# Counting graph edges on VectorE: window staging moved off GpSimd, digit sums moved three groups later

## What is computed

```python
deg = maximum(segment_sum(ones, dst), 1); d = deg ** -0.5
h = relu(layernorm(x))
feat = h
for i in range(10):
    agg = segment_sum(feat[src] * (d[dst] * d[src])[:, None], dst)
    feat = (agg * 0.9 + 0.1 * h) * r[i] + (1 - r[i]) * feat
x = x + feat
emb = relu(layernorm(x))
for _ in range(4):
    m = (emb @ W_msg.T + b_msg).reshape(n, 4, 128)
    emb = gru(segment_sum(m[src, edge_type], dst), emb, ...)
return x + emb
```

## Time and profile before

| | us |
|---|---|
| median of three runs | 2482.77 (2481.85 to 2486.41) |
| the profiled execution's own time | 2481.51 |
| its span in the trace | 2480.0 |
| PE busy | 2164.4 (87%) |
| VectorE (DVE) busy | 1392.8 (56%) |
| ScalarE (ACT) busy | 502.2 (20%) |
| GpSimd (POOL) busy | 236.5 (10%) |

### The profile page before, as it was taken

The page is one execution under the profiler, slowest core; times in us unless marked ns, Lnnn a source line. Parts: engine busy times, 40 slices in busy tenths (PEclk is TensorE's granted clock), DMA queues, the critical chain, the costliest instruction groups (busy, mean ns, idle before and its releaser), DMA issues.

```text
span 2480.0 us, 40786 instructions
## 1 busy us (share of the span) xinstructions
PE 2164.4 (87%) x14375; PEld 1409.1 (57%) x14886; DVE 1392.8 (56%) x2707; ACT 502.2 (20%) x1119; POOL 236.5 (10%) x517
## 2 busy tenths in 40 slices
PE   1645555499999999999799999999999999999997
PEld 1323222388998989888544465444654446544464
DVE  6878788677777777777732246322464224642243
ACT  0868778510000000000310012100121000210000
POOL 1756556100000000000000000000000000000000
PEclk9656556599999999999899999999999999999998
DMA  2000000000000000003200000000000000000001
GB/s 75 12 32 22 32 21 29 30 24 2 2 2 2 2 2 2 2 2 109 85 1 1 1 1 1 1 1 1 1 1 1 1 1 1 1 1 1 1 1 52
DMA packets 22185, 34.31 MB, mean 14 GB/s; under 512 B 2450, under 2 KB 18442, under 8 KB 21469
## 3 DMA queue, kind: packets, MB, share of 16 engines
q1 hardware_dynamic: 19025, 30.56, 3.6%
q10 hardware_dynamic: 2944, 0.93, 0.2%
HBM read 18.04 MB, written 13.45 MB: 13 GB/s over the span
## 4 chain that ended last, share of the span: by engine, by line
PE 77%; DVE 8%; ACT 6%; issue 4%; DMA 2%; ACTq 1%; DVEq 1%; POOL 1%; POOLq 0%
PE ps L852 42%; PE ps L771 26%; PE ps L804 3%; ACT weighed L516 3%; PE ps L792 2%; ACT packed L509 2%; ACT words L498 1%; ACTq L489 1%; DVE marks L1038 1%; DVE dig L1066 1%; DVE big L1068 1%; DMA big<-in_L_gnn_w_hh 1%; DMA x_after_hops<-x 1%; PE ps L712 1%; PE ps L668 1%
## 5 line engine op out<-in xcount | busy, mean ns | idle before, releaser
L852 PE MATMUL ps<-slots,m_parts 125*128 125x500 fp8e4 (+1 forms) x5600 | 1083.8, 353 | 1.4 <-DVE slots L1338 1.0
L852 PEld LDWEIGHTS ps<-slots,m_parts 125*128 125x128 f16 x5600 | 546.5, 98 | 488.2 <-issue 0.8
L771 PE MATMUL ps<-parts,big 125*128 125x256 f16 x6125 | 669.6, 273 | 6.2 <-DVEq L1385 4.0
L771 PEld LDWEIGHTS ps<-parts,big 125*128 125x128 fp8e4 x6125 | 591.2, 98 | 63.5
L1338 DVE TENSOR_SCALAR slots<-big 128x3200 int32<-128x3200 int32 (+1 forms) x112 | 244.1, 2183 | 280.4 <-PE ps L852 280.4
L668 PE MATMUL ps<-hot_pair,weighed 125*128 125x228 f16 x1000 | 209.9, 358 | 207.6 <-ACT weighed L516 121.7
L668 PEld LDWEIGHTS ps<-hot_pair,weighed 125*128 125x128 f16 x1000 | 113.4, 120 | 303.9 <-ACT weighed L516 266.3
L516 ACT ACTIVATE weighed<-marks,win_w 125x128 f16<-125x128 f16 x625 | 195.5, 389 | 121.0 <-DVE marks L1038 119.9
L1440 DVE SCALAR_TENSOR_TENSOR r_parts<-ps,over,r_parts 128x500 f16<-128x500 f32 (+1 forms) x28 | 19.1, 683 | 230.1 <-ACT r_parts L586 230.1
L1447 DVE SCALAR_TENSOR_TENSOR gate_r<-ps,over,gate_r 128x500 f32<-128x500 f32 (+1 forms) x28 | 19.1, 682 | 228.6 <-PE ps L804 228.6
L462 ACT ACTIVATE rs<-rs 125x25 f32<-125x25 f32 x3 | 0.7, 224 | 716.1 <-DVE rs L917 716.1
(11 more groups left out here) (203 smaller groups left out, 1329.8 us busy)
## 6 DMA issues: line engine op xcount, KB each, us to landing
packed_counts<-packed SPq DMA_DIRECT2D x16, 625.0 KB, 2.9
big<-packed_counts SPq DMA_DIRECT2D x4, 1600.0 KB, 7.3
big<-packed_counts SPq DMA_DIRECT2D x3, 1200.0 KB, 6.5
hd<-in_x SPq DMA_DIRECT2D x1, 1562.5 KB
x_again<-in_x SPq DMA_DIRECT2D x1, 1562.5 KB
x_after_hops<-x SPq DMA_DIRECT2D x1, 1562.5 KB
big<-x_after_hops SPq DMA_DIRECT2D x1, 1562.5 KB
out<-big SPq DMA_DIRECT2D x4, 250.0 KB
```

What stands on the lines that cost most here:

```text
L771: last = pe.matmul(ps[:, n % RING, 0:2 * F], tot_f8[0:Q, c, a, :], both((parts0, parts1)[par], a), start=a == 0, stop=a == TILES - 1)
L852: last = pe.matmul(ps[:, k % 2, 0:SIZES[k] * Q], m_parts[0:Q, a, h, t * F:(t + 1) * F], slots_f8[0:Q, t % 2, 0:SIZES[k], a, 0:Q], start=a ...
```

## The change

GpSimd's `stage_window` and its loop are gone. Two tables are made once by ScalarE, before the counting: `tab_two` (both tables of `tab`, each element twice) and `tab_w` (the weights in f32). VectorE loads `lo` itself, forms `win_key`, and reads places and weights in `tab_two` by the register's address; ScalarE loads `lo` too, and reads its weight per partition in `tab_w` by the register's address. VectorE's wait for `s_wst` is now one for its own key operation, behind `marks`. The digit sums move: `sum_digits(blk - 2)` stands behind the second group of block `blk`, ten groups behind the last one-hots that it sums; blocks 0 and 1 of one-hots stand ahead of the loop, blocks 2 to 13 in three turns of it, and 14 and 15 behind it. `sum_digits(14)` now comes behind the statistics, right ahead of `sum_digits(15)`. ScalarE parts its lanes one group earlier (j = 2, 3, 4).

```diff
@@ buffers
-            win_place = sb("win_place", [128, DEPTH, W, 2], F16, b)
-            win_f = sb("win_f", [128, DEPTH, W, 2], F16, b)
-            win_w = sb("win_w", [128, DEPTH, W], F32, b)
+            tab_two = sb("tab_two", [128, 2, PAD, 2], F16, b)
+            tab_w = sb("tab_w", [128, PAD], F32, b)
@@ gpsimd
-            def stage_window(q, b):
...
-            with pool.Fori(0, Q // DEPTH) as i:
-                for j in range(DEPTH):
-                    stage_window(DEPTH * i + j, j)
-            for q in range(Q // DEPTH * DEPTH, Q):
-                stage_window(q, q % DEPTH)
@@ scalar
             act.wait_ge(s_prep, 1)
             act.wait_ge(s_wout, 1)
 
+            act.wait_ge(s_trc, 3)
+            for j in range(2):
+                ins = act.activation(tab_two[0:CH, j, :, :], tab[0:CH, j, :].rearrange("p (k o) -> p k o", o=1)
+                                     .broadcast_to([CH, PAD, 2]), ACT.Copy)
+            ins.then_inc(s_two, 1)
+            act.activation(tab_w[0:CH, :], tab[0:CH, 1, :], ACT.Copy).then_inc(s_two, 1)
...
+            act.wait_ge(s_two, 2)
+
             def weigh(q, b):
+                lo = act.value_load(windows[0:1, ds(q, 1)], min_val=0, max_val=NCH)
                 act.wait_ge(s_marks, q + 1)
                 for w in range(WA):
                     act.activation(weighed[0:CH, b, w, :], marks[0:CH, b, w, :], ACT.Copy,
-                                   scale=win_w[0:CH, b, w:w + 1]).then_inc(s_weighed, 1)
+                                   scale=tab_w[0:CH, ds(lo + w, 1)]).then_inc(s_weighed, 1)
...
-                    if 3 <= j < 3 + LANES and turn_before is not None:
-                        part_lane(turn_before, 1 - b, j - 3, 16 * turn_before + BQ * (1 - b) + BQ - 1)
+                    if 2 <= j < 2 + LANES and turn_before is not None:
+                        part_lane(turn_before, 1 - b, j - 2, 16 * turn_before + BQ * (1 - b) + BQ - 1)
...
-            part_lane(NB // 2 - 1, 0, 2, BQ * (NB - 1) - 1)
@@ vector, onehots
                 many = dve.value_load(windows[0:1, ds(q + MANY, 1)], min_val=0, max_val=NCH)
-                dve.wait_ge(s_wst, q + 1)
+                lo = dve.value_load(windows[0:1, ds(q, 1)], min_val=0, max_val=NCH)
+                weights_from = nc.s_assert_within(lo + WA, 0, PAD - WD)
+                TT(win_key[0:CH, b, :, :], keys[0:CH, ds(lo, W)].rearrange("p (w o) -> p w o", o=1).broadcast_to([CH, W, 2]),
+                   q_off[0:CH, ds(q, 1)].rearrange("p (w o) -> p w o", o=1).broadcast_to([CH, W, 2]),
+                   ALU.subtract).then_inc(s_wst, 1)
                 dve.wait_ge(s_hot_used, q + 1)
...
                 TT(by_two(marks[0:CH, b, :, :], 128), row(iota_row[0:CH, :], W, 128),
-                   each(win_place[0:CH, b, :, :], W, 128), ALU.is_equal).then_inc(s_marks, 1)
+                   each(tab_two[0:CH, 0, ds(lo, W), :], W, 128), ALU.is_equal).then_inc(s_marks, 1)
+                dve.wait_ge(s_wst, q + 1)
                 TT(by_two(hot_pair[0:CH, b, :, :], KP), row(iota_pair[0:CH, :], W, KP),
                    each(win_key[0:CH, b, :, :], W, KP), ALU.is_equal).then_inc(s_pairs, 1)
                 dve.wait_ge(s_marks, q + 1)
                 TT(by_two(weighed[0:CH, b, WA:W, :], 128), by_two(marks[0:CH, b, WA:W, :], 128),
-                   each(win_f[0:CH, b, WA:W, :], WD, 128), ALU.mult).then_inc(s_weighed_d, 1)
+                   each(tab_two[0:CH, 1, ds(weights_from, WD), :], WD, 128), ALU.mult).then_inc(s_weighed_d, 1)
@@ vector, order
-            for j in range(BQ):
-                onehots(j, j % DEPTH)
-            def block_of(blk, b):
-
-                for j in range(BQ):
-                    onehots(BQ * (blk + 1) + j, j % DEPTH)
-                    if j == BQ - 2:
-                        sum_digits(blk, b)
+            dve.wait_ge(s_two, 2)
+
+            def block_of(blk, b, n=BQ):
+
+                for j in range(n):
+                    onehots(BQ * blk + j, j % DEPTH)
+                    if j == 1:
+                        sum_digits(blk - 2, b)
+
+            for j in range(2 * BQ):
+                onehots(j, j % DEPTH)
...
-            sum_digits(NB - 2, 0)
             dve.wait_ge(s_wout, 1)
...
             root_of(stats[0:Q, :, 1], EPS)
+            sum_digits(NB - 2, 0)
             sum_digits(NB - 1, 1)
             one_over_root(rstd[0:Q, :], 1)
```

More of the change, by code:

```diff
@@ L269, in build @@
         s_wst, s_pairs, s_hot_used = sem("window_staged"), sem("pair_onehots_made"), sem("onehots_used")
+        s_two = sem("tables_doubled")
         s_marks, s_weighed = sem("place_onehots_made"), sem("place_onehots_weighed")
@@ L1043, in onehots @@
                 TT(by_two(weighed[0:CH, b, WA:W, :], 128), by_two(marks[0:CH, b, WA:W, :], 128),
-                   each(win_f[0:CH, b, WA:W, :], WD, 128), ALU.mult).then_inc(s_weighed_d, 1)
+                   each(tab_two[0:CH, 1, ds(weights_from, WD), :], WD, 128), ALU.mult).then_inc(s_weighed_d, 1)
                 with dve.If(many > 0):
-                    lo = dve.value_load(windows[0:1, ds(q, 1)], min_val=0, max_val=NCH - 1)
+                    first = dve.value_load(windows[0:1, ds(q, 1)], min_val=0, max_val=NCH - 1)
                     with dve.Fori(0, many) as j:
@@ L1049, in onehots @@
                         dve.wait_ge(s_more_used, dve.snap(made))
-                        col = nc.s_assert_within(lo + j + W, 0, PAD - 1)
+                        col = nc.s_assert_within(first + j + W, 0, PAD - 1)
                         TS(win_x[0:CH, 0:1], keys[0:CH, ds(col, 1)], q_off[0:CH, ds(q, 1)], None, ALU.subtract)
@@ L1100, in onehots_general @@
                            ALU.is_equal, ALU.mult).then_inc(s_more_g, 1)
-            for j in range(BQ):
-                onehots(j, j % DEPTH)
-            def block_of(blk, b):
-                for j in range(BQ):
-                    onehots(BQ * (blk + 1) + j, j % DEPTH)
-                    if j == BQ - 2:
-                        sum_digits(blk, b)
-            with dve.Fori(0, (NB - 2) // ROUND) as i:
+            dve.wait_ge(s_two, 2)
[5 more added lines that the diff above has]
+            for j in range(2 * BQ):
+                onehots(j, j % DEPTH)
+            TURNS = (NB - 3) // ROUND
+            with dve.Fori(0, TURNS) as i:
                 steps.loop(i, 4 * ROUND)
                 for k in range(ROUND):
-                    block_of(ROUND * i + k, k % 2)
-            steps.done((NB - 2) // ROUND)
-            for blk in range((NB - 2) // ROUND * ROUND, NB - 2):
+                    block_of(ROUND * i + k + 2, k % 2)
+            steps.done(TURNS)
+            for blk in range(TURNS * ROUND + 2, NB - 1):
                 block_of(blk, blk % 2)
-            for q in range(BQ * (NB - 1), Q):
-                onehots(q, q % DEPTH)
-            sum_digits(NB - 2, 0)
+            block_of(NB - 1, 1, Q - BQ * (NB - 1))
             dve.wait_ge(s_wout, 1)
```

## The result

The changed kernel takes 2541.6 us (2540.6 to 2543.0, four runs) against 2482.3 us of the kernel before in the same session: a ratio of 1.0236, 95% interval 1.0218 to 1.0254. The forecast was 2554 in a range of 2505 to 2600. The profiled execution's span is 2539.1 us, 59.1 more than before.

What follows compares the result with a forecast made beforehand. The prediction took VectorE's queue as the bound, 3.01 us a window: one-hots 471 us from a start at 58, tail 18.0, degrees at 546 instead of 473.2. That is +72.8 on 2481.5, 2554 us, range 2505 to 2600.

Steps and rivals of the forecast that it cites:

- The circle of the queue: VectorE's queue work per counting window, `marks` to `marks`: 1.80 us plus 1.21 added makes 3.01, against 1.89 of datapath.
- the value loads: In VectorE's queue, per window: the existing load takes 0.71 us and the added load of `lo` another 0.71.
- `lo + WA` with its assertion: Added register arithmetic per window in VectorE's queue: 0.103 us, assertion 0.023, gaps of 0.035 behind each; 0.20 us.
- Slow fetches: Behind the branch in VectorE's queue: one window of five is 0.3 us longer, together 7 us.
- Digit windows: The 14 counting windows with a digit sum: no wait for ScalarE, 9.47 us each, 6.46 over a plain window.
- All of the one-hots: VectorE's counting stage: 376 for 125 windows, less 8, plus 90 digit sums, 6 loop turns, 7 slow fetches: 471 us.
- The start: First `marks` no longer waits for POOL's key operation: about 58 us instead of 64.45, 6.5 us gained.
- The tail: Last one-hots to PE's degrees: statistics 7.1, digit sums 5.4 and 5.5, no wait for ScalarE: 18.0 us.
- ScalarE costs nothing: ScalarE's added load and addresses, 1.3 us a window, stay hidden at 2.2 us, showing only with VectorE near 2 us.
- Rival 1: Counting stage: register work stays hidden and VectorE's datapath decides, windows of 2.0 us, 2431 us in all; chance 0.08.
- Rival 2: VectorE's queue runs on past the wait for `marks`: 2.4 us a window, no change, about 2485 us; chance 0.06.
- Rival 3: Instruction fetch becomes the bound as the loop body grows: 3.5 us a window, 2615 us; chance 0.04.

Runs made afterwards that it cites:

- experiment 2: Changed kernel with the old order of digit sums and lanes, so only the register addressing is left: 2549.4 us, ratio 1.0266.
- experiment 4: Changed kernel with both value loads of the next group placed ahead of the wait for `marks`: 2461.2 us, ratio 0.9910.
- experiment 7: Kernel before with only ScalarE reading weights by register address, GpSimd staging three tensors, old order: 2490.3 us, ratio 1.0023.
- experiment 1: Kernel before with only the new order: digit sums ten groups behind, lanes one group earlier, GpSimd stages kept: 2457.2 us, ratio 0.9895.
- experiment 5: Kernel before with the new order and ScalarE reading weights by register address, GpSimd staging three tensors: 2451.2 us, ratio 0.9868.
- experiment 10: Kernel before with one more value load per group on VectorE, its result unused: 2529.5 us, ratio 1.0181.
- experiment 3: Changed kernel with one more value load per group on VectorE, its result unused: 2624.6 us.
- experiment 6: Changed kernel with the next group's loads ahead of the wait for `marks`, one load instruction filling both registers: 2441.1 us, ratio 0.9829.

## Why the prediction was right

The change costs 59.1 us where 72.8 was forecast. The mechanism is the one forecast; the difference is in the sizes of terms.

- **The circle of the queue** was the bound, as forecast. Of its terms the value loads were 0.71 us each; wait, weights' address and branch 0.39, where 0.24 + 0.13 was forecast; the key's and the places' address 0.32 (0.33 forecast). The step that failed is the second in the list of queue work, "`lo + WA` with its assertion", 0.20 us. No such instruction stands in the trace; the addition went into the weights' address, which takes 0.086 us instead of 0.059, and no assertion was made. Without the term the sum is 2.81 us; 2.82 was measured. That is 0.19 x 107 = 20 us too much in the sum.

```profile
L1036 DVEq FUSED_REGOPS  x125: 80/86/94, 56.3 to 511.9; - x125
```

- **Slow fetches** I had at 7 us. The mean of the plain windows is 2.900 against 2.82 of the usual ones, although the first 16 are shorter (2.57): 33 windows of 3.0 us or more bring about 12 us. The step had the right kind and was too small. A term that the forecast did not have is the window of 4.46 us where the code behind the loop begins (`marks` at 449.99, then 454.45), 1.6 us over its neighbours. That these gaps are fetches of instructions is my reading; the rows name no cause.
- **Digit windows**: 9.47 forecast, 9.21 measured, again the missing assertion and little else. They wait for nobody, as forecast. That is 4 us too much.
- **All of the one-hots** took 457.6 us where the sum, less its last 1, had 470: 24 us too much by the assertion, about 7 too little by the slow windows and the one of 4.46 us; the other 5 are spread over small differences that were not taken apart.
- **The start**: 58 forecast, 55.6 measured. 2.0 us of the 8.9 gained are luck of this execution: the copies into `tab`, ahead of all that the change touches, began at 29.64 where it was 31.63 before. In experiments 2 and 4 they began at 31.36 and 31.21, and the first `marks` stands at 56.84 and 57.19, so the forecast was about 1 us high.
- **The tail**: 18.0 us forecast from the last one-hots to the degrees, 530.97 - 513.14 = 17.8 measured; ScalarE was done at 522.0, ahead of the sum that needs it, which starts at 525.5. What lies behind was forecast unchanged and is 1.5 us longer.
- **ScalarE costs nothing**: right in this kernel, and for the reason given, but the estimate of 2.2 us a window was a shade high (2.04), and its consequence, that it shows as soon as VectorE is near 2 us, is experiment 7.
- **Rival 1** (register work hidden) needed added work under 0.2 us; it was 2.82 - 1.80 = 1.02, and the windows grew by 0.93. **Rival 2** (the queue runs past the wait; by its own sum, PE at 481, its time is 2489 and not about 2485) is not borne out: in the chain above no queue instruction of the next group starts before `marks` has ended at 207.70. In all 125 windows the first queue instruction behind the wait, the weights' address, starts 0.04 us after the end of `marks`, and in the kernel before the branch, which stands there behind the third instruction, 0.05 us after it. The Trainium skill (Perfetto Trace Analysis, "Per-engine timelines") has the sequencer free once an instruction is pushed. The trace agrees for an instruction whose wait is met (experiment 4, load at 210.53, `hot_pair` at 210.99) and not for one whose wait isn't. It is not the branch that holds the queue, as the address in front of it is held too; whether it is the wait itself or something tied to it was not taken apart. **Rival 3** had the kind right, a fifth of its price.

## What to carry to other kernels

Price the queue as an engine of its own: a register loaded from SBUF was 0.71 us on VectorE here, an address made from a register about 0.1, and they are free only while the datapath has more to do than the queue *behind the wait that holds it*. If register work must be done, do it in front of the wait: the same two loads cost 80 us in one place and not in the other. And when a wait is taken away, look up which one is next; the reordered digit sums were worth 26 us with the old windows, of the 43 that the wait itself showed, and 8 in the slower ones. And before an engine is blamed for a wait, look whether the waiting queue had got there at all: of the idle time put down to GpSimd a third in experiments 1 and 5, and three quarters in experiment 10, was VectorE's own queue.

## What was not expected

- One load of two words took 0.512 us, against 0.305 for one word, 504 bytes apart in one partition; the register operations per word stay.
- In experiment 3 the granted clock of TensorE was 1.00 between 60 and 500 us (2.4 GHz), and in the changed kernel 0.51 (1.2 GHz for nearly all of it), with the same matmuls; yet the window of experiment 3 is longer by its load and not shorter by anything: TensorE's clock is worth nothing in this stage. The changed kernel's own executions agree: with a mean clock of 0.99 they took 2540.6 and 2543.0 us, with 0.89 and 0.90 2540.6 and 2542.6. The rows of that stretch, of the changed kernel and of experiment 3 (busy us and count of PE, PEld, DVE, ACT, POOL, then PEclk); TensorE did fewer matmuls in the second, 816 for 969:

```profile
60.00:500.00 440.00, 219.35 (x969) 117.71 (x969) 327.59 (x552) 295.65 (x765) 0.00 (x0) 0.51 0.05 22
```
```profile
60.00:500.00 440.00, 174.23 (x816) 107.53 (x816) 275.06 (x462) 255.96 (x643) 0.00 (x0) 1.00 0.05 19
```

- GpSimd's first key operation stood 7.6 us in issue at the start, and 7.0 to 7.6 in each kernel that has it. To be rid of it gives about 6 us of the start (first `marks` at 57.19 in experiment 4, 63.23 in experiment 1), of the 16 us that experiment 6 is under experiment 1.
